# A two-layer graph network kernel: comparison constants read from PSUM, casts split by size

## The reference

```python
h = max(layernorm(x), 0)
msg = edge_weight[:, None] * (h[dst] @ W_i + h[src] @ W_j + edge_attr @ W_e)
x = x + segment_sum(msg, dst) + h @ W_self
h = max(layernorm(x), 0)
def sage(h, W_l, b_l, W_r):        # mean over incoming edges of h[src]
    return segment_sum(h[src], dst) / max(count, 1)[:, None] @ W_l.T + b_l + h @ W_r.T
x = x + log_softmax(sage(relu(sage(h, W1_l, b1_l, W1_r)), W2_l, b2_l, W2_r))
```

## Time and profile before

| | us |
|---|---|
| median of 3 runs | 1550.66 (1547.23 to 1553.08) |
| the profiled execution | 1547.76 |
| its span, first to last instruction | 1544.8 |
| busy: PE, PEld | 1218.4, 991.2 |
| busy: DVE, ACT | 1048.9, 713.1 |
| busy: POOL | 1076.7 |
| mean granted PE clock | 0.943 |

### The profile page before, as it was taken

One profiled execution on the slowest core, in us unless ns is written; L12 is line 12 of the kernel. 1 busy time (PEld: TensorE's weight loads), 2 busy tenths in 40 slices (PEclk: granted clock), 3 DMA queues, 4 the chain that ended last, 5 costly groups with the idle time before them and its releaser, 6 DMA issues. The chain is left out here.

```text
span 1544.8 us, 27421 instructions
## 1 busy us (share of the span) xinstructions
PE 1218.4 (79%) x9615; PEld 991.2 (64%) x9615; DVE 1048.9 (68%) x2113; ACT 713.1 (46%) x1202; POOL 1076.7 (70%) x1048
## 2 busy tenths in 40 slices
PE   0057888898888889888876498798998888979887
PEld 0035777677777777767754277677776666757665
DVE  7659577988888788877787265455454555666565
ACT  3124344655556445544677143343343443434344
POOL 4877776777777777776777637777774077777770
PEclk9998999999999999999999599999999999989999
DMA  8358555756576466654577556566565665665663
GB/s 248 99 153 234 138 169 165 216 149 190 162 218 176 141 180 191 185 140 131 186 213 226 160 141 196 161 174 187 157 178 146 181 193 149 188 190 161 182 171 88
DMA packets 320573, 266.98 MB, mean 173 GB/s; under 512 B 32393, under 2 KB 298020, under 8 KB 320436
## 3 DMA queue, kind: packets, MB, share of 16 engines
q1 hardware_dynamic: 272708, 189.44, 41.9%
q0 software_dynamic: 33616, 69.34, 17.2%
q10 hardware_dynamic: 14112, 6.43, 1.5%
HBM read 212.08 MB, written 53.00 MB: 172 GB/s over the span
## 5 line engine op out<-in xcount | busy, mean ns | idle before, releaser
L845 POOL DMA_INDIRECT Dt<-h_d,idx x624 | 628.3, 1007 | 200.7 <-issue 188.7
L1451 POOL DMA_INDIRECT Dg<-g_d,idx x390 | 418.3, 1072 | 204.3 <-issue 147.0
L1412 PE MATMUL pc<-Kt,hi 128*128 128x512 f32 (+1 forms) x980 | 397.9, 410 | 13.7 <-issue 6.0
L1412 PE MATMUL pc<-Kt,lo 128*128 128x512 f32 (+1 forms) x980 | 380.5, 392 | 0.0
L1345 DVE CAST Kt<-Ut 128x2048 fp32r<-128x2048 uint8 (+3 forms) x168 | 235.7, 1410 | 55.0 <-PE pc L1412 46.3
L1240 ACT ACTIVATE Cb<-pc 128x784 uint8<-128x784 f32 x304 | 240.2, 823 | 49.6 <-PE pc L1228 47.3
L1412 PEld LDWEIGHTS pc<-Kt,hi 128*128 128x128 f32 x980 | 192.0, 196 | 55.5 <-issue 16.6
L1412 PEld LDWEIGHTS pc<-Kt,lo 128*128 128x128 f32 x980 | 191.8, 196 | 32.2
L1347 ACT ACTIVATE Kt<-Ut 128x1536 fp32r<-128x1536 uint8 (+3 forms) x112 | 181.5, 1622 | 62.6 <-PE pc L1412 52.9
L1202 DVE TENSOR_TENSOR Jt<-ps,keyT 128x1568 bf16<-128x1568 bf16 x204 | 196.5, 969 | 4.5 <-PE pc L1228 1.4
L1228 PE MATMUL pc<-Jt,Rt 128*128 128x196 bf16 x1216 | 148.2, 251 | 41.8 <-ACT Cb L1240 34.6
(11 more groups left out here) (152 smaller groups left out, 1552.3 us busy)
## 6 DMA issues: line engine op xcount, KB each, us to landing
Ut<-c_d SPq DMA_DIRECT2D x126, 448.0 KB, 3.9
Dt<-in_ea SPq DMA_DIRECT2D x208, 192.0 KB
c_d<-Cb SPq DMA_DIRECT2D x38, 784.0 KB
Dq<-in_ea SPq DMA_DIRECT2D x77, 192.0 KB
Dt<-h_d,idx POOLq DMA_INDIRECT x624
g_d<-ht ACTq DMA_DIRECT2D x98, 64.0 KB
r_d<-rt SPq DMA_DIRECT2D x98, 64.0 KB
sp<-g_d SPq DMA_DIRECT2D x14, 448.0 KB, 4.4
```

What stands on the lines that cost most here:

```text
L845: e.indirect_dma_start(Dt[:, s, t, 0:128], None, h_d, bass.IndirectOffsetOnAxis(idx[:, c:c + 1], 0))\
L1412: last = e.matmul(pc[:, k % 2, 0:n], part[:, q, :], Kt[:, t % NK, j - q0, 0:n], start=(x == 0 and t % 2 == 0 and j == 0 and part is hi), s ...
L1451: e.indirect_dma_start(Dg[:, s, t, :], None, (g1_d, g2_d)[L], bass.IndirectOffsetOnAxis(idx[:, c:c + 1], 0)).then_inc(s_gg[s], 16)
```

## The change

Four things move. (1) `iop` is a copy of the numbers 0..127 in PSUM bank 3, and each `OH`, `Sg`, `Sw` and `Sq` compares with it and no longer with `con` in SBUF. (2) `slot_weights` no longer does two instructions over 12 tiles, but 12 `tensor_scalar` of 32 numbers, each with two operands that are one number a partition (`drel` and `ew`). (3) For own blocks `wp` is copied, for each block, to bank 3 (`wpp`), and the three multiplications read it there. (4) ACT casts all units of four source blocks and DVE all of three. Besides, `give_r` of the last layer uses bank 2 instead of 3, and `slots` makes the copy.

```diff
--- before.py
+++ after.py
@@ -228,6 +228,8 @@
         ident = con[:, CI:CI + 128]
         iota = con[:, CIO:CIO + 128]
         ip = ps[3][:, :].bitcast(BF16)[:, 0:196]
+        iop = ps[3][:, 128:256]
+        wpp = ps[3][:, :].bitcast(BF16)[:, 512:704].rearrange("p (a w two) -> p a w two", w=32, two=2)
 
         cnt = sb("cnt", [128, NWC], F32)
         c1f = sb("c1f", [128, NWC], F32)
@@ -722,6 +724,7 @@
             e.tensor_copy(i196[:, 0:128], iota)
             link(e, e.tensor_scalar(i196[:, 128:196], iota[:, 0:68], 128.0, None, ALU.add))
             e.tensor_copy(ps[3][:, 0:98], i196[:, :].bitcast(F32))
+            link(e, e.tensor_copy(iop, iota))
             e.memset(Dq[:, :, :, 128:129], 1.0)
             link(e, e.memset(Dt[:, :, :, 256:257], 1.0))
             e.sem_inc(s_one, 1)
@@ -819,12 +822,11 @@
                             A["ea"][e0:e0 + 384, :].rearrange("(p j) f -> p j f", j=3)).then_inc(sems[s], 16)
 
         def slot_weights(e, S, s, g):
-            n = group_tiles(g)
-            T = [128, n, 32]
-            link(e, e.tensor_tensor(S[:, s, 0:n, :], con[:, CI32:CI32 + 32].unsqueeze(1).broadcast_to(T),
-                                    drel[:, 12 * g:12 * g + n].unsqueeze(2).broadcast_to(T), ALU.is_equal))
-            return e.tensor_tensor(S[:, s, 0:n, :], S[:, s, 0:n, :],
-                                   ew[:, 12 * g:12 * g + n].unsqueeze(2).broadcast_to(T), ALU.mult)
+            for t in range(group_tiles(g)):
+                c = 12 * g + t
+                last = e.tensor_scalar(S[:, s, t, :], iop[:, 0:32], drel[:, c:c + 1], ew[:, c:c + 1],
+                                       ALU.is_equal, ALU.mult)
+            return last
 
         def load_group(g):
             s = g % ND
@@ -944,7 +946,7 @@
                     e.wait_ge(s_p2, n - 1)
                 for i, g in enumerate(gs):
                     r = rows_in(g)
-                    last = e.tensor_scalar(OH[0:r, n % 2, i, :], iota[0:r, :], 128.0 * b, rowid[0:r, g:g + 1],
+                    last = e.tensor_scalar(OH[0:r, n % 2, i, :], iop[0:r, :], 128.0 * b, rowid[0:r, g:g + 1],
                                            ALU.add, ALU.is_equal)
                 last.then_inc(s_oh, 1)
 
@@ -1133,7 +1135,7 @@
 
         def give_r(L, b):
             m = turn_of[L, b]
-            o = (0, 3)[L]
+            o = (0, 2)[L]
             bank = hand(o, s_pq, m + 1)
 
             def pe(e):
@@ -1195,8 +1197,11 @@
                     if m >= 2:
                         e.wait_ge(s_cm, 2 * (octs.index((k - 2, True)) + 1))
                     own = R[:, 8 * (i % 2):8 * (i % 2) + 8, :]
+                    if m % 4 == 0:
+                        pair = wp[:, :, 8 * m:8 * m + 32, :].rearrange("p a w two -> p a (w two)").bitcast(F32)
+                        link(e, e.tensor_copy(ps[3][:, 256:352].rearrange("p (a w) -> p a w", w=32), pair))
                     for part, to in ((1, RW[:, m % 2, 0, :, :]), (2, RW[:, m % 2, 1, :, :]), (0, own)):
-                        e.tensor_tensor(pairs(to), pairs(own), each(wp[:, part, 8 * m:8 * m + 8, :], 64), ALU.mult)
+                        e.tensor_tensor(pairs(to), pairs(own), each(wpp[:, part, 8 * (m % 4):8 * (m % 4) + 8, :], 64), ALU.mult)
                 if i >= NJ:
                     e.wait_ge(s_cm, 2 * (i - NJ + 1))
                 e.tensor_tensor(pairs(Jt[:, i % NJ, :, :]), every(ip, 8), each(keyT[:, 8 * k:8 * k + 8, :], 98),
@@ -1306,7 +1311,7 @@
 
 
 
-        unit_by = ["act" if t % 5 in (1, 3) else "dve" for t in range(4 * NI)]
+        unit_by = [("act", "dve")[t % 2] for t in range(4 * NI)]
         unit_nth = [unit_by[:t + 1].count(unit_by[t]) for t in range(4 * NI)]
 
         def unit_done(e, t):
@@ -1457,7 +1462,7 @@
                     e.wait_ge(s_p2, NB)
                 if z >= NDG:
                     e.wait_ge(s_g1, z - NDG + 1)
-                e.tensor_tensor(Sg[:, s, 0:n, :], con[:, CI32:CI32 + 32].unsqueeze(1).broadcast_to(T),
+                e.tensor_tensor(Sg[:, s, 0:n, :], iop[:, 0:32].unsqueeze(1).broadcast_to(T),
                                 drel[:, 12 * g:12 * g + n].unsqueeze(2).broadcast_to(T), ALU.is_equal)\
                     .then_inc(s_sg, 1)
 
@@ -1516,7 +1521,7 @@
                     e.wait_ge(s_g2, y - 1)
                 for i, g in enumerate(gs):
                     n = rows_in(g)
-                    last = e.tensor_scalar(OH[0:n, y % 2, i, :], iota[0:n, :], 128.0 * b, rowid[0:n, g:g + 1],
+                    last = e.tensor_scalar(OH[0:n, y % 2, i, :], iop[0:n, :], 128.0 * b, rowid[0:n, g:g + 1],
                                            ALU.add, ALU.is_equal)
                 last.then_inc(s_go2, 1)
```

## The result

The changed kernel takes 1577.87 us (median of 4, 1576.23 to 1588.91) beside 1548.95 for the kernel before: ratio 1.0202 [1.0161, 1.0242]. A second set gave 1583.79 beside 1549.62, ratio 1.0217 [1.0184, 1.0250]. It is slower by 2%, where 1540 was forecast. Stage 2 did what the prediction said; stage 1 got more than twice as much longer as forecast.

The account below looks back on a forecast made before the run. POOL's gathers were taken to bound stage 2, and stage 1 only at its end. Stage 1 +30 and stage 2 -40 make -10 on 1547.8, so 1538, and 1540 as median; the range of 8 in 10 was 1510 to 1570.

Parts of the forecast that it names:

- The bound of stage 2: Stage 2, the last 665 us: POOL's gathers with their issue gaps set the pace of both layers.
- the casts as its cause: Stage 2: DVE casts of 2048 numbers hold POOL's gathers up; POOL's surplus there is 50 us.
- its gain: Stage 2: 40 us less, bounds 20 and 50.
- The price of an operand: DVE's short slot_weights instructions: each per-partition operand costs about 0.06 us, the second as well; twelve take 2.75 us.
- the 104 us of DVE: DVE in 100:720: short slot_weights instructions add 1.7 us in each of 61 groups; bounds 9 and 107.
- `OH` from PSUM: DVE in 100:720: each OH costs 0.065 us more at one number a cycle, 9 us in all.
- L1199's successor: Own blocks' three weight multiplications on DVE: stay at 0.60 us each, two numbers a cycle, with PSUM input.
- 622 + 16 + some 15 of waits that stay: Stage 1: DVE's busy time, hand-over and remaining waits make 653 us of 620, so 33 us longer, called 35.
- the wait of 50.9 us for PE at own blocks: DVE in 100:720: its largest wait, taken to shrink as DVE comes later.
- the second rival: Stage 1, plain blocks: own-block waits can't be used, 50 us stay, 68 us longer, 1573 us in all; chance 0.20.
- The 5 us that POOL should have given back: End of stage 1: gathers without their surplus make it 5 us shorter.
- a falling clock: PE: named as a way to be wrong, if its clock falls with denser work; no size given.

Follow-up runs that it names:

- h1: Kernel before with only the casts split anew (ACT four source blocks, DVE three): 1516.11 us beside 1549.38, ratio 0.9787.
- h3: Changed kernel with the edge weight left out of Sw and Sq (constant 1 as second operand): 1548.70 us, ratio 0.9987.
- h2: Changed kernel with the old slot_weights (two instructions over 12 tiles): 1515.64 us, ratio 0.9800.
- e3: Kernel before with the twelve short instructions alone: ratio 1.0237, on a slow chip where the kernel before took 2139.01 us.
- i3: Changed kernel with a second, unused short instruction ahead of each of Sw's: ratio 1.0854, beside a kernel before of 2096.93 us.
- i4: h2 with Sw and Sq's compared numbers from PSUM and OH from SBUF: ratio 1.0536, beside a kernel before of 2096.93 us.

## Why the prediction was wrong

**Right.** The bound of stage 2, the casts as its cause (h1), and its gain: 38 for 40. PE's waits for gathered rows there are 9.3 and 12.2 us, from 20.6 and 29.9. The price of an operand, 0.06, and that the second costs as well (h3); the twelve take 1.57 us more than the pair and not 1.7, so the 104 us of DVE are 96. `OH` from PSUM, in the changed kernel's timeline, one and three of them:

```profile
559.92 0.34 DVE L949 TENSOR_SCALAR OH<-ps,rowid 128x128 f32<-128x128 f32 x1
...
723.01 0.86 DVE L949 TENSOR_SCALAR OH<-ps,rowid 128x128 f32<-128x128 f32 x3
```

They start (0.86 - 0.34) / 2 = 0.26 us apart, from 0.196: 0.065 more, as taken. L1199's successor stays at two numbers a cycle with the weight from PSUM, 0.60 apart, as the prediction took it from the earlier trace rows. Against the perf-mode tier table on the page "VectorE: DVE Perf Modes" of the Trainium skill, which gives one a cycle, the trace decides.

**The step that failed** is the sum for stage 1: "622 + 16 + some 15 of waits that stay". 55 us of waits stayed in 100:720, and the step from the idle to a new length was wrong in kind, not only in that number. It treated the wait of 50.9 us for PE at own blocks as slack that work added anywhere in stage 1 could use; 27.7 us of it stayed. Cutting stage 1 into own stretches (from the first to the last instruction that writes `RW` in an own block) and plain stretches (between them) shows why. Of h2, the sums over 13 own stretches and over the 13 plain ones behind them (us, then busy PE, PEld, DVE, ACT, POOL):

```profile
sum 191.10, PE 174.72 PEld 158.01 DVE 159.04 ACT 83.44 POOL 138.27; mean PE 13.44 PEld 12.15 DVE 12.23 ACT 6.42 POOL 10.64
```

```profile
sum 406.50, PE 333.22 PEld 272.85 DVE 336.10 ACT 230.35 POOL 295.54; mean PE 25.63 PEld 20.99 DVE 25.85 ACT 17.72 POOL 22.73
```

and of the changed kernel:

```profile
sum 194.90, PE 174.33 PEld 157.51 DVE 174.89 ACT 79.85 POOL 132.30; mean PE 13.41 PEld 12.12 DVE 13.45 ACT 6.14 POOL 10.18
```

```profile
sum 461.80, PE 358.39 PEld 289.29 DVE 408.37 ACT 234.30 POOL 289.82; mean PE 27.57 PEld 22.25 DVE 31.41 ACT 18.02 POOL 22.29
```

These are 12 own blocks, for the second is cut in two: its middle stands among the plain stretches, in h2 and in the changed kernel (single rows give us, the same five, then clock, DMA share, GB/s):

```profile
151.00:167.70 16.70, 16.70 (x152) 15.21 (x145) 4.71 (x9) 1.70 (x4) 12.74 (x14) 0.93 0.71 205
```

```profile
166.40:184.40 18.00, 18.00 (x152) 16.50 (x145) 7.91 (x28) 1.72 (x4) 11.92 (x13) 0.86 0.64 179
```

It holds the longest of the waits at `RW`. Counted where it belongs, the own stretches take 207.8 us in h2 and 212.9 in the changed kernel, the plain ones 389.8 and 443.8.

In the own stretches DVE gets 19 us more and the length rises by 5: there idle time was used up, as forecast. In the plain stretches DVE gets 69 us more and the length rises by **54**. DVE was busy 85% there and PE 81%; now 90% and 77%. Neither was full and neither is: each waits in turn for a fresh result of the other, and 15 us of DVE's 58 idle were used up. That is near to the second rival ("the 51 us at own blocks can't be used there"), given 0.20 and 1573 us, whose own sum was 622 + 16 + 50, 68 us longer; measured are 1578 to 1584. Its decision point, a stage 1 over 45 us longer, is passed at 69. The range given ended at 1570, below this rival's own number. The 5 us that POOL should have given back are not seen, for it waits for PE.

**A second part of the size.** PE's own time in the plain stretches rose by 24 us. The records of its instructions add up to 3205 and 3262, so up to 6 us may be more work and 18 are a slower PE, 0.104 instead of 0.099 us each. One stretch of h2, of the changed kernel and of the kernel before:

```profile
573.40:611.60 38.20, 32.07 (x318) 26.88 (x316) 32.85 (x66) 24.11 (x41) 28.95 (x31) 1.00 0.67 195
```

```profile
628.50:669.90 41.40, 34.29 (x318) 28.42 (x316) 39.01 (x106) 24.28 (x41) 30.36 (x34) 0.92 0.61 184
```

```profile
568.60:608.80 40.20, 34.02 (x315) 27.87 (x313) 32.41 (x66) 23.92 (x41) 30.45 (x33) 0.92 0.64 186
```

The same 318 instructions take 2.2 us more of PE at a granted clock of 0.92 (a mean over the two levels, 2.4 and 1.2 GHz) instead of 1.00. But the kernel before has 0.92 here as well, and is 2.0 us longer than h2 with no more of DVE; against it the changed kernel has 6.6 us more of DVE and is 1.2 longer. In another stretch, h2 and then changed, both run at 1.00:

```profile
372.00:401.70 29.70, 24.01 (x257) 20.46 (x255) 25.61 (x59) 18.21 (x34) 21.29 (x23) 1.00 0.57 161
```

```profile
410.20:442.60 32.40, 24.73 (x260) 20.81 (x259) 30.15 (x88) 18.22 (x34) 20.25 (x22) 1.00 0.53 150
```

There 4.5 us more of DVE make 2.7 us of length with no change of clock (in the last stretch, at 0.95 in both, 3.6 us more make only 0.2). So DVE's time can lengthen a stretch by itself, and from the one stretch above a lower clock seems to as well; how the 54 us divide between them no run here tells. In 100:720 the clock falls along with the added time, 0.97 in h2, 0.94 in h3 and 0.92 in the changed kernel, so the equal slopes don't separate them. The prediction named a falling clock as a way to be wrong, but for denser work, and gave it no price; it fell where PE is less busy (499 of 620 us, from 533).

**Not shown.** The short instructions alone on an ordinary chip (e3 ran on the slow one), a slope below 59 us or beyond 111 (i3 too), what share of the length is the clock's and why it fell, and whether i4 beats h1 and h2. Of what was timed on ordinary chips, h1 and h2 are the best, 1516 us, and can't be told from each other; h1 needs one line.

## What to carry to other kernels

Where two in-order engines are each 80 to 85% busy and feed each other, added work on one is not absorbed by its idle time: here it showed at 0.56 us per us, for 59 us of it as for 111. Cut the stage into stretches of unlike shape before adding idle time up, since slack in one can't be spent in another, and price the clock that the idle partner may lose. Taking a wait away where it stands may gain nothing: here it came back at other places.

On DVE, twelve instructions of 32 numbers cost two and a half times what two of 384 do (2.63 and 1.06 us), though they touch half as many numbers. And change one thing at a time: one part of this change was worth 33 us, another cost 62.

## What the runs showed of the hardware

- On DVE a per-partition operand costs 0.06 us in an instruction of 32 numbers, measured for the second (starts 0.158 and 0.219 apart; durations 242 and 302 ns in h3 and the changed kernel) and estimated for the first.
- bf16 `tensor_tensor` with its second input in PSUM runs at two numbers a cycle (1024 numbers, starts 0.60 us apart, 680 ns), as from SBUF, and did not hold POOL up: a gather that started at 721.40 beside such ones took 0.94 us, where the earlier trace rows have 2.68.
- Casts of 2048 numbers from SBUF to SBUF on DVE lengthen the gather beside them, by 0.6 us in the earlier trace rows and by 1.0 at another place (1.94 us for the gather at 1395.20 in the kernel before); with them on ACT the mean gather of stage 2 is 955 ns (h1), from 1072.
- Some chips ran the same kernel in 2097 to 2147 us instead of 1549, with stretches of up to 12 us in which PE stands and whose cause no view names, and a granted clock of 0.80 to 0.84, and there the sign of an edit's effect was not the same.
